# A three-layer graph attention stack: VectorE's range checks, row maxima and statistics at later blocks

## The reference

```python
h = x @ W
e = leaky_relu((h @ a_src)[src] + (h @ a_dst)[dst], 0.2)
m = segment_max(e, dst)
ex = exp(e - m[dst])
z = segment_sum(ex, dst)
out = segment_sum((ex / z[dst])[:, None] * h[src], dst) + b
```

## Time and profile before

| | |
|---|---|
| median of 3 runs | 685.88 us (685.61 to 686.31) |
| the profiled execution | 684.96 us |
| its span, first to last instruction | 683.1 us |
| TensorE busy | 591.5 us, 87% |
| VectorE busy | 639.8 us, 94% |
| ScalarE busy | 484.3 us, 71% |
| GpSimd busy | 460.1 us, 67% |
| mean granted TensorE clock | 0.963 |

### The profile page before, as it was taken

The page is one execution under the profiler, slowest core; times in us unless marked ns, Lnnn a source line. Parts: engine busy times, 40 slices in busy tenths (PEclk is TensorE's granted clock), DMA queues, the critical chain, the costliest instruction groups (busy, mean ns, idle before and its releaser), DMA issues.

```text
span 683.1 us, 13824 instructions
## 1 busy us (share of the span) xinstructions
PE 591.5 (87%) x5571; PEld 573.1 (84%) x5571; DVE 639.8 (94%) x911; ACT 484.3 (71%) x719; POOL 460.1 (67%) x448
## 2 busy tenths in 40 slices
PE   1729865899978999999999899999989989999994
PEld 1628755789878999899989799999988979999994
DVE  3999999999999989999987998999998899999993
ACT  0416544656969688887666788989886698888891
POOL 5579101889928565775954675858598678697883
PEclk9978986899999999999999999999999999999999
DMA  2410002000000000000100100000010010110001
GB/s 70 119 56 2 1 7 6 35 2 1 20 1 1 20 1 20 2 1 8 26 14 1 27 1 20 2 19 1 8 20 20 1 27 6 35 32 8 20 1 42
DMA packets 22325, 12.07 MB, mean 18 GB/s; under 512 B 12393, under 2 KB 20055, under 8 KB 22255
## 3 DMA queue, kind: packets, MB, share of 16 engines
q1 hardware_dynamic: 21455, 9.85, 6.3%
q0 software_dynamic: 800, 1.26, 0.6%
HBM read 9.47 MB, written 1.64 MB: 16 GB/s over the span
## 4 chain that ended last, share of the span: by engine, by line
DVE 51%; PE 29%; issue 8%; DMA 5%; POOL 4%; ACT 2%; POOLq 0%; DVEq 0%
PE ps L1813 21%; DVE scratch L951 20%; DVE ps L1067 15%; DVE scratch L1149 5%; DMA xr<-in_x 3%; POOL scratch L751 2%; DVE ps L1069 2%; DVE ps L1079 1%; PE ps L1866 1%; PE ps L1821 1%; PE ps L1844 1%; DVE scratch L1067 1%; DMA gathered<-in_edges,start_i 1%; DVE gathered L1149 1%; PE ps L1780 1%
## 5 line engine op out<-in xcount | busy, mean ns | idle before, releaser
L1813 PE MATMUL ps<-hB,scratch 125*125 125x129 f32 x3450 | 404.5, 276 | 21.1 <-DVE scratch L1149 17.6
L1813 PEld LDWEIGHTS ps<-hB,scratch 125*125 125x125 f32 x3450 | 390.9, 189 | 28.4 <-DVE scratch L1149 22.6
L751 POOL TENSOR_TENSOR scratch<-scratch,C 125x625 f32<-125x625 f32 x239 | 304.3, 1285 | 113.0 <-ACT scratch L1569 110.9
L1067 DVE SCALAR_TENSOR_TENSOR ps<-C,a_unit,ps 125x625 f32<-125x625 fp8e3 x330 | 275.4, 866 | 2.3
L1567 ACT ACTIVATE scratch<-gathered,r_neg 125x625 f32<-125x625 f32 x219 | 176.6, 806 | 20.3 <-PE ps L1813 19.2
L1569 ACT ACTIVATE scratch<-scratch,r_src 125x625 f32<-125x625 f32 x219 | 178.9, 817 | 7.1
L1452 ACT ACTIVATE C<-ps 125x1000 fp8e3<-125x1000 f32 x80 | 78.2, 1001 | 77.9 <-PE ps L1780 77.7
L1780 PE MATMUL ps<-scratch 128*128 128x125 bf16 x1250 | 93.4, 239 | 32.7 <-DVE scratch L951 30.7
L1780 PEld LDWEIGHTS ps<-scratch 128*128 128x128 bf16 x1250 | 85.7, 108 | 39.9 <-DVE scratch L951 37.8
L1149 DVE SCALAR_TENSOR_TENSOR scratch<-ps,r_src,C 125x625 f32<-125x625 f32 x121 | 104.1, 860 | 5.4 <-PE ps L1803 5.3
L951 DVE TENSOR_TENSOR scratch<-key_lo,ps 128x4096 bf16<-128x4096 bf16 (+3 forms) x41 | 89.3, 2178 | 0.0
(11 more groups left out here) (195 smaller groups left out, 444.6 us busy)
## 6 DMA issues: line engine op xcount, KB each, us to landing
gathered<-g_lines SPq DMA_DIRECT2D x15, 305.2 KB
xr<-in_x SPq DMA_DIRECT2D x1, 1562.5 KB
out<-xr SPq DMA_DIRECT2D x4, 312.5 KB
edge_sb<-in_edges SPq DMA_DIRECT2D x1, 805.7 KB
gathered<-ext_lines SPq DMA_DIRECT2D x5, 122.1 KB
w<-in_W SPq DMA_DIRECT2D x2, 128.0 KB
out<-xr SPq DMA_DIRECT2D x1, 187.5 KB
out<-xr SPq DMA_DIRECT2D x1, 125.0 KB
```

The costliest lines, as they stand in the source:

```text
L751: g.tensor_tensor(slot[s], slot[s], C5[:, q % NC, s, :], ALU.mult).then_inc(pool_done, 1)
L1067: v.scalar_tensor_tensor(dest, counts, unit[:, s:s + 1], top, ALU.min, ALU.max).then_inc(S.top_done, 1)
L1813: last = mm(ps[0:P, acc_at(t):acc_at(t) + HW], A[:, P * t:P * (t + 1)], feat, start=opens and t in (0, 3), stop=closes, skip_group_check=True)
```

## The change

Nothing is computed otherwise; the same instructions stand at other places.

- In chunk 1 all that is left from chunk 0 moves by two blocks: TensorE's transposes from behind block 14 to behind block 16, VectorE's chain and sums by two, the rest by one or two.
- In chunks 6 to 9 VectorE's chain moves from blocks 2 and 3 to 4 and 5, its sums from block 4 to 6, and its statistics from block 9 to 10. GpSimd's, ScalarE's and TensorE's places stay.
- The range checks move from block 2 to block 17 of chunks 6 and 11.

```diff
+        MODE_AT = 17
         FIRST_LAYER = (None,
-                       At(14, (15, 15, 16, 16), 16, (17, 17, 18), None, (23,), (21, 23, 27), (23, 25, 29), 25, 27),
+                       At(16, (17, 17, 18, 18), 18, (19, 19, 20), None, (24,), (23, 25, 29), (25, 27, 31), 27, 29),
...
-                 At(1, (2, 2, 3, 3), 4, (4, 4, 4), (9, 9), (11, 15), (15, None, 17), (14, 16, 19), None, None),
+                 At(1, (4, 4, 4, 5), 5, (6, 6, 6), (10, 10), (11, 15), (15, None, 17), (14, 16, 19), None, None),
...
-                    if L and c == 1 and s == 2:
+                    if L and c == 1 and s == MODE_AT:
                         over_nodes(2 * L, ext_all, all_ready)
```

More of the change, by code:

```diff
@@ L400, in gat_stack_kernel @@
         USUAL = (At(1, (3, 4, 5, 6), 6, (8, 9, 10), None, (14,), (12, 15, 21), (14, 17, 23), 18, 20),
-                 At(1, (2, 2, 3, 3), 4, (4, 4, 4), (9, 9), (11, 15), (15, None, 17), (14, 16, 19), None, None),
+                 At(1, (4, 4, 4, 5), 5, (6, 6, 6), (10, 10), (11, 15), (15, None, 17), (14, 16, 19), None, None),
                  At(1, (3, 4, 5, 6), 6, (8, 9, 10), None, (14, 17, 20), (None,) * 3, (None,) * 3, None, None))
         BEFORE_LAST = (At(1, (3, 4, 5, 6), 6, (8, 9, 10), None, (14,), (12, 14, 19), (13, 16, 21), 17, 18),
-                       At(1, (2, 2, 3, 3), 4, (4, 4, 4), (9, 9), (11, 15), (15, None, 17), (14, 16, 19), None, None))
+                       At(1, (4, 4, 4, 5), 5, (6, 6, 6), (10, 10), (11, 15), (15, None, 17), (14, 16, 19), None, None))
         TURN = (At(None, (1, 1, 2, 2), 3, (3, 3, 3), None, (11,), (7, 9, 13), (9, 12, 15), 11, 13),
```

## The result

| | before | after |
|---|---|---|
| median | 685.57 us, 10 runs (684.21 to 686.31) | 688.65 us, 10 runs (687.32 to 690.60) |
| the profiled execution | 684.96 us | 687.32 us |
| its span | 683.1 us | 685.6 us |

The change makes the kernel slower: ratio 1.0048, 95% interval 1.0037 to 1.0059. The forecast was 689.3 us, with 0.80 for slower.

The account below looks back on a forecast made before the run. VectorE (busy 94%) and TensorE (87%) were both taken as full where nothing disturbs them. The terms 2.7 - 1.2 + 0.4 + 1.55 = +3.45 us on a median of 685.88 gave 689.3 us, range 686.5 to 691.0.

Parts of the forecast that it names:

- Chunk 1, +2.7: Chunk 1: transposes behind blocks 15 and 16 end late, VectorE's reduction waits 2.5 us, everything behind is 2.7 us later.
- lower bound: Chunk 1: if TensorE kept full clock, the transposes would end at 225.2 and the term would be -1.4 us.
- upper one: Chunk 1, upper bound: if the idle stretch also lengthens the slow one by a block's time, the term is +3.8 us.
- Chunk 6, -1.2: Chunk 6: range checks leave the way of block 4's product, and VectorE gains its wait at chunk 7's first product, 1.2 us.
- Chunks 7 and 8, +0.2 each: Chunks 7 and 8: later `back` delays ScalarE's `kappa` and the row maxima and normalisation behind it, 0.2 us longer each.
- Chunk 9, +1.55: Chunk 9: two tops stand ahead of the chain to GpSimd's scaling, whose gapless work ends last, costing 1.55 us.
- Chunk 11, nothing: Chunk 11: checks leave the way of block 4's product, but VectorE has no wait through chunk 13, so nothing is gained.
- The waits removed count: Rival, chunks 6 to 9: TensorE's waits end late, so VectorE's 3.1 us of waits go, giving 682.8; chance 0.08.
- GpSimd gives way in chunk 9: Rival, chunk 9: the later `rz` is hidden and the 1.51 us wait stays, so that term is nothing: 687.8; chance 0.16.
- Nearly nothing: Rival: chunk 1's late transposes cost only what chunk 6 returns, the rest being too small to tell: 685.9; chance 0.12.
- The clock falls in chunk 9 too: Rival, chunk 9: after TensorE's 3.2 us stand, blocks 11 to 15 run slow, costing 1.1 us more: 690.4; chance 0.18.

Follow-up runs that it names:

- tops14: The changed kernel with the first top's five transposes in chunk 1 back at block 14, VectorE's chain staying at blocks 17 and 18: 685.24 us.
- kappa6: The changed kernel with ScalarE's kappa at block 6 instead of 5 in chunks 6, 7 and 8: 687.54 us.
- checks_only: The kernel before with only the range checks moved, from block 2 to block 17 of chunks 6 and 11: 682.74 us, ratio 0.9957.
- second_only: The kernel before with only VectorE's chain, sums and statistics moved in chunks 6 to 9, range checks still at block 2: 686.04 us, ratio 1.0014.
- without_first: The changed kernel with chunk 1 laid out as in the kernel before: 685.29 us, ratio 0.9996.
- rz_early: checks_only with chunk 9's chain on VectorE one block shorter, the inverse and rz at block 3 instead of 4: 683.93 us.

## Why the prediction was right, and where it was not

**Chunk 1, +2.7: right in mechanism and size (+2.83).** The steps came out within 0.4 us: the reduction waited 2.19 us (forecast 2.5), the transposes ended at 226.86 (227.0), block 18's product started at 227.97 (228.1), and TensorE waited 0.94 for it (1.0) and 0.60 for the next two (1.0). tops14 shows by one number that the loss goes with the transposes' place, though its trace had full clock there. The forecast's lower bound, a gain of 1.4 us at full clock, is not tested, and in its upper one a longer slow stretch is right: kappa6's trace has +4.12 us where +3.8 was named. So the good agreement in size rests on the short slow stretch of this execution. The cheap alternative, that chunk 2's 1.89 us of slack would absorb it, fell as argued: VectorE waits there for TensorE itself, and the wait grew to 2.40.

**Chunk 6, -1.2: mis-sized (-2.15).** The step that failed is the sentence "More is not to be had, since the work on VectorE is unchanged." The order of the work was counted, its durations were taken as fixed. The checks took 2.47 us because 1.05 of them was line 1020 standing for GpSimd's product; in the changed kernel they run from 407.91 to 409.50, 1.59 us. The wait of 1.19 us and these 0.88 make 2.07 of the 2.15 us. The row was in the view that was read, between the ones that were quoted: a 1x1 comparison of 1.20 us beside neighbours of 0.14 to 0.41.

**Chunks 7 and 8, +0.2 each: right (+0.17 each),** and so is the reason, ScalarE's row maxima behind a late `kappa`: moving kappa by one block turned the loss into a gain of 0.45 and 0.32 us against before. ScalarE's wait for `back` was 2.99 us, not about 2, but what follows kept to the forecast: the normalisation started 20.22 us after the chunk's first product (20.3).

**Chunk 9, +1.55: right (+1.47).** GpSimd's scaling waited 2.35 us (forecast 2.4), TensorE 3.01 before block 11 (3.2), VectorE 2.77 before chunk 10 (3.1).

**Chunk 11, nothing: right.** All that follows chunk 10's first product differs by 0.06 us.

**The rivals.** "The waits removed count" (682.8) fell in chunk 1, where the transposes ended at 226.86 and not by 226.4, and in chunk 9, where GpSimd is last. That checks_only reaches the same time is chance: 1.05 us of its gain are line 1020's, which no wait of the rival holds. "GpSimd gives way in chunk 9" (687.8) fell with the wait of 2.77 us. "Nearly nothing" fell with the interval, which lies above 1. "The clock falls in chunk 9 too" came true in its first half. In four traces with the new layout of chunk 9 (second_only, without_first, tops14 and kappa6) the granted clock is 0.50 after the stand before block 11. This stretch of second_only shows it (length, busy by engine, clock):

```profile
503.50:504.80 1.30, 1.30 (x8) 1.30 (x8) 1.30 (x3) 1.24 (x2) 1.22 (x3) 0.50 0.00 0
```

Its price was too high: chunk 9 takes 36.14 to 36.30 us with the fall and 35.99 without, so 0.15 to 0.3 us and not 1.1. TensorE waits for GpSimd at block 15 anyway (0.93 us in the trace after), and half clock fills that wait: in the four traces it is gone.

**The sum.** By the traces it is 2.5 us, by the medians 3.1, forecast 3.45. The traces' 2.5 us fall short by the 0.95 us of chunk 6. That the medians come within 0.4 us of the forecast is in part luck, since no term of the sum stands for what the other runs had more than the profiled one. The profiled execution was the fastest of its ten. kappa6 shows what the others may hold: its chunk 1, which has the same program, took 36.54 instead of 35.25 us because the lower clock lasted longer. The same two stretches of chunk 1, first of the kernel after, then of kappa6:

```profile
224.90:226.20 1.30, 1.30 (x12) 1.30 (x11) 0.00 (x0) 1.19 (x2) 0.00 (x0) 0.82 0.00 0
226.20:227.50 1.30, 1.30 (x14) 1.30 (x14) 0.61 (x1) 0.44 (x1) 0.78 (x1) 1.00 0.00 0
```

```profile
224.90:226.20 1.30, 1.30 (x8) 1.30 (x8) 0.00 (x0) 1.27 (x2) 0.00 (x0) 0.50 0.00 0
226.20:227.50 1.30, 1.30 (x8) 1.30 (x8) 0.00 (x0) 0.17 (x1) 1.05 (x1) 0.50 0.00 0
```

With 1.3 us more the changed kernel's 687.32 would be 688.6, its median. The nine others had a lower mean clock (0.957 to 0.963, against 0.968 in the profiled one), which fits; but two of them, at 0.963, were within 0.35 us of it, and no trace of them exists, so it is not shown.

## What to carry to other kernels

A wait of a less loaded engine is worth only what the fullest engine later waits for; work that is put in front of something on which another engine's queue stands (`back` for ScalarE, `rz` for GpSimd, the transposes for VectorE) is paid for at once if that engine has nothing in hand. When an order is moved, look also for instructions that take far longer than their shape says: they stand for something, and a new place can free them (-1.05 us) or catch others (+1.1 us). A change of three parts with one sum can hold a gain: here one of its parts alone is 2.7 us faster, and with the transposes of chunks 2 and 3 moved the other way and kappa moved along 4.5, of which kappa and its order are 0.3.

## What the runs showed of the hardware

- A VectorE instruction of one element took from 0.15 to 1.20 us, by how much of a GpSimd product of 1.24 us was left when it started. Both its inputs are in SBUF. One of 125x5 with both inputs there took 1.27 us instead of 0.17 in the same way (rz_early). VectorE's products of 125x625, which read one operand from PSUM, took 0.86 us beside the same products of GpSimd.
- The lower of the two clock levels, 1.2 GHz, began in an idle stretch of TensorE in chunk 1 and lasted 3.4 us in the trace after (about 222.0 to 225.4, idle for 3.92 us) and 6.8 us in that of kappa6 (about 221.0 to 227.9, idle for 3.33 us), with the same program there. In checks_only, where TensorE's order in chunk 1 is that of before, a stretch of 6.8 us made chunk 1 1.18 us longer; one of 3.4 us in the kernel before cost nothing against none in without_first (32.42 and 32.43 us). After the stand of 3.0 us in chunk 9 the clock fell in kappa6 and stayed in the kernel after. One trace prices one outcome of this.
